# Gathering the last states of node groups by counts loaded into registers, in a seven-round graph network on one core

## The reference

```python
x = _layernorm(x + L0(x, edge_index))                        # normalised sum over the edges of a node
x = _layernorm(x + L1(x, edge_index, edge_attr_32, ...))     # two transformer convolutions, softmax per node
x = _layernorm(x + L2(x, weight, edge_weight1, src, dst, edge_type_16))   # relation matrices, weighted sum
x = _layernorm(x + L3(x, edge_index, W1, b1, W2, b2))        # three edge convolutions, maximum per node
```

## Time and profile before

| | us |
|---|---|
| median of 3 runs | 8052.2 (8051.64 to 8053.5) |
| the profiled execution | 8052.15 |
| its span, first to last instruction | 8050.2 |
| POOL busy | 5546.3 (69%) |
| PE busy (matmuls) | 4278.3 (53%) |
| DVE busy | 2503.7 (31%) |
| ACT busy | 2071.7 (26%) |

### The profile page before, as it was taken

One profiled execution on the slowest core, in us unless ns is written; L12 is line 12 of the kernel. 1 busy time (PEld: TensorE's weight loads), 2 busy tenths in 40 slices (PEclk: granted clock), 3 DMA queues, 4 the chain that ended last, 5 costly groups with the idle time before them and its releaser, 6 DMA issues.

```text
span 8050.2 us, 123362 instructions
## 1 busy us (share of the span) xinstructions
PE 4278.3 (53%) x24036; PEld 2775.3 (34%) x24036; DVE 2503.7 (31%) x4334; ACT 2071.7 (26%) x6406; POOL 5546.3 (69%) x5874
## 2 busy tenths in 40 slices
PE   3444435555555555566333326666646666466664
PEld 2333324444444444442222213333323333233332
DVE  5444435555535555531333331111111111111112
ACT  1111114444424444431111111111111111111111
POOL 6777757666637666633777757777767777577776
PEclk9999999999999999999999996565555656556565
DMA  5566647777736767622222224444444544344443
GB/s 144 150 150 150 150 102 151 150 151 151 152 87 151 152 152 151 149 61 93 60 59 59 59 60 109 111 112 112 101 96 112 112 111 111 86 112 111 111 111 87
DMA packets 2187581, 925.65 MB, mean 115 GB/s; under 512 B 1607262, under 2 KB 2070694, under 8 KB 2181094
## 3 DMA queue, kind: packets, MB, share of 16 engines
q1 hardware_dynamic: 1078982, 458.38, 23.1%
q10 hardware_dynamic: 921120, 272.38, 14.6%
q0 software_dynamic: 187392, 193.93, 13.3%
HBM read 657.22 MB, written 266.58 MB: 115 GB/s over the span
## 4 chain that ended last, share of the span: by engine, by line
PE 45%; issue 36%; POOL 9%; DVE 4%; DMA 4%; ACT 2%; ACTq 0%; DVEq 0%; POOLq 0%
POOL edges_a L906 8%; PE ps L1213 8%; PE ps L1205 7%; PE ps L1136 6%; PE ps L1132 6%; PE ps L1148 5%; PE ps L1197 4%; PE ps L1122 3%; DMA edges_a<-src_table,idx 3%; PE ps L584 2%; PE ps L1113 1%; PE ps L635 1%; PE ps L577 1%; POOL edges_a L913 1%; PE ps L1181 1%
## 5 line engine op out<-in xcount | busy, mean ns | idle before, releaser
L906 POOL DMA_INDIRECT edges_a<-src_table,idx x4040 | 3821.5, 946 | 1519.6 <-issue 1165.5
L913 POOL DMA_INDIRECT edges_a<-src_table,idx x1616 | 1524.6, 943 | 768.5 <-issue 448.8
L1341 DVE TENSOR_TENSOR_SCAN st<-pen,st,ps 128x512 f32<-128x512 f32 x300 | 383.9, 1280 | 2591.9 <-PE ps L1205 2591.7
L1132 PE MATMUL ps<-ident,edges_a 128*128 128x128 f32 x1212 | 563.5, 465 | 1173.1 <-issue 1024.6
L1213 PE MATMUL ps<-ident,st 64*128 64x64 f32 (+2 forms) x4444 | 926.2, 361 | 430.3 <-issue 395.1
L1122 PE MATMUL ps<-ident,edges_a 128*64 128x128 f32 x1616 | 419.1, 415 | 1255.1 <-DVE edges_a L1359 672.7
L1213 PEld LDWEIGHTS ps<-ident,st 64*128 64x128 f32 (+2 forms) x4444 | 704.9, 215 | 1043.9 <-issue 997.0
L1341 DVE TENSOR_TENSOR_SCAN st<-edges_a,st,ps 64x512 f32<-64x512 fp8e4 x402 | 511.2, 1272 | 874.9 <-issue 475.8
L1132 PEld LDWEIGHTS ps<-ident,edges_a 128*128 128x128 f32 x1212 | 219.3, 181 | 1428.8 <-issue 1266.4
L1040 ACT ACTIVATE edges_a<-ps,b 128x512 f32<-128x512 f32 x303 | 208.2, 687 | 1912.6 <-PE ps L1136 1912.6
L1122 PEld LDWEIGHTS ps<-ident,edges_a 128*64 128x64 f32 x1616 | 216.4, 158 | 1337.7 <-issue 1256.5
(11 more groups left out here) (189 smaller groups left out, 3531.6 us busy)
## 6 DMA issues: line engine op xcount, KB each, us to landing
states_sum<-hb ACTq DMA_DIRECT2D x1010, 128.0 KB
win_sb<-dst_table SPq DMA_DIRECT2D x1616, 72.8 KB
edges_a<-src_table,idx POOLq DMA_INDIRECT x5656
states_att<-hb ACTq DMA_DIRECT2D x404, 194.0 KB
win_sb<-dst_table ACTq DMA_DIRECT2D x1212, 48.0 KB
win_sb<-dst_table SPq DMA_DIRECT2D x1212, 48.0 KB
dst_b<-in_dst_row SPq DMA_DIRECT2D x50, 1024.0 KB, 5.7
sel<-onehots SPq DMA_DIRECT2D x303, 128.0 KB
```

What stands on the lines that cost most here:

```text
L906: pool.indirect_dma_start(rows[:, s, j * D:(j + 1) * D], None, srcs[q.r], bass.IndirectOffsetOnAxis(ap=idx[:, s, j:j + 1], axis=0))\
L913: pool.indirect_dma_start(xe_a[:, s, j * KA:j * KA + D], None, srcs[q.r], bass.IndirectOffsetOnAxis(ap=idx_a[:, s, j:j + 1], axis=0))\
L1132: nc.tensor.matmul(bank(TURNED, s)[:, at_j], rows[:, s, j * P:(j + 1) * P], ident[:, :], is_transpose=True, start=True, stop=False)
L1341: nc.vector.tensor_tensor_scan(st[0:w, s % V, :], d0, d1, init, op0, op1).then_inc(q.st_ready.sem, 1)
```

## The change

The change has three parts.

1. A table of counts. DVE makes `group_ends` with 17 small operations ahead of the masks: for each of the first six groups, how many rows of four chunks must be stored until the group's last edge is covered, times 16 (for MAX rounds times 32), once cut off at the larger and once at the smaller number of uses that a slot has in a round. For the halves of a MAX round a group of the first half needs its own rows, a group that reaches into the second half while it begins in the first needs all of them, and a group of the second half needs its rows there.
2. In rounds 2 to 6 POOL, in place of one wait ahead of the 25 gathers, loads two of these counts into registers ahead of each of the first six groups and waits for the four slots with them. Ahead of the last group it waits for all chunks, as before.
3. In rounds 0 and 1 POOL waits for all chunks ahead of group 0 as before (and again, in vain, ahead of group 6).

```diff
                 kw = KA if q.kind == ATT else D
-                for s in range(U):
-                    wait(pool, (q.st_stored[s], 16 * q.per_step * ((q.steps - s + U - 1) // U)))
+                each, most, least = 16 * q.per_step, -(-q.steps // U), q.steps // U
+                pool.wait_ge(ends_made, ENDS_MADE)
                 for g, (b0, nb) in enumerate(GROUPS):
+                    if g < G - 1 and q.r > 1:
+                        ends = [nc.values_load(group_ends[P - 1:P, int(q.kind == MAX), e:e + 1],
+                                               engines=[mybir.EngineType.Pool], min_val=each, max_val=each * m)
+                                for e, m in ((g, most), (G - 1 + g, least))]
+                        wait(pool, *[(q.st_stored[s], ends[0] if s < q.steps % U else ends[1]) for s in range(U)])
+                    elif g == G - 1 or not g:
+                        wait(pool, *[(q.st_stored[s], each * ((q.steps - s + U - 1) // U)) for s in range(U)])
                     for b in range(b0, b0 + nb):
...
+            half, full = float(CH * EC), float(-(-CH // U))
+            begins, finals = edges_le[:, 0:GB * (G - 1):GB], edges_le[:, GB:NB:GB]
...
+            for to, off in ((all_rows, 0.0), (second_rows, half)):
+                end_op(nc.vector.tensor_scalar(to, finals, -1.0 - off, 0.0, ALU.add, ALU.max))
+                end_op(nc.vector.tensor_scalar(to, to, 1.0 / (U * EC), 1.0, ALU.mult, ALU.add))
+                end_op(nc.vector.tensor_copy(up_to, to))
+                end_op(nc.vector.tensor_copy(to, up_to))
+            end_op(nc.vector.tensor_scalar(first_rows, finals, half, full, ALU.is_gt, ALU.mult))
+            end_op(nc.vector.tensor_tensor(first_rows, first_rows, all_rows, ALU.add))
+            end_op(nc.vector.tensor_scalar(split_rows, begins, half, full, ALU.is_le, ALU.mult))
+            end_op(nc.vector.tensor_tensor(second_rows, second_rows, split_rows, ALU.add))
+            end_op(nc.vector.tensor_tensor(second_rows, second_rows, first_rows, ALU.min))
+            for i, (of, steps, each) in enumerate(((all_rows, C, 16.0), (second_rows, CH, 32.0))):
+                for j, most in enumerate((-(-steps // U), steps // U)):
+                    end_op(nc.vector.tensor_scalar(group_ends[:, i, j * (G - 1):(j + 1) * (G - 1)], of, float(most), each,
+                                                   ALU.min, ALU.mult))
```

More of the change, by code:

```diff
@@ L133, in gnn_kernel @@
         dinv = sb("dinv", [P, NB])
+        group_rows = sb("group_rows", [P, 4, G - 1])
+        group_ends = sb("group_ends", [P, 2, 2 * (G - 1)], i32)
         xn = sb("xn", [P, NB, D])
@@ L231, in gnn_kernel @@
         agg_ready = [sem(f"agg_ready{g}") for g in range(G)]
+        ends_made = sem("ends_made")
         LN = ["sum", "mean", "centred", "square", "var", "rstd", "norm"]
@@ L427, in pre_tiles @@
             return 2 + sum(nb + 2 for _, nb in GROUPS[:g + 1]) + 3 * max(g - LATE + 1, 0)
+        ENDS_MADE = 17
         LATE = 3
@@ L1302, in _, with end_op @@
             assert made[0] == PRE_SCALED
+            done = [0]
+            def end_op(ins):
+                done[0] += 1
+                ins.then_inc(ends_made, 1)
+                dve.wait_ge(ends_made, done[0])
+            half, full = float(CH * EC), float(-(-CH // U))
+            begins, finals = edges_le[:, 0:GB * (G - 1):GB], edges_le[:, GB:NB:GB]
+            all_rows, first_rows, second_rows, split_rows = (group_rows[:, i, :] for i in range(4))
+            up_to = group_ends[:, 0, 0:G - 1]
+            for to, off in ((all_rows, 0.0), (second_rows, half)):
[12 more added lines that the diff above has]
+                                                   ALU.min, ALU.mult))
+            assert done[0] == ENDS_MADE
             nc.vector.tensor_copy(tile_last[:, 0:whole].unsqueeze(2), tile_dst[:, 0:whole, P - 1:P])
```

## The result

| | before | after |
|---|---|---|
| median of 5 runs, us | 8053.5 (8051.64 to 8054.84) | 8005.59 (8003.41 to 8006.57) |
| the profiled execution, us | 8052.15 | 8005.16 |
| its span, us | 8050.2 | 8003.2 |

The ratio is 0.9941, with an interval of 0.9926 to 0.9955: 48 us less, where 49.6 were forecast and the median of after lies 3 us above the forecast. None of them ran on the chip of the result, so what is said of that chip rests on the two traces, before and after.

A forecast was written before the change was run, and what follows sets the result against it. POOL's gathers of source rows pace the chunks; the change fills POOL's idle seams between rounds. Gains 12.5 + 9.2 + 9.5 + 9.5 + 8.9 = 49.6 us off 8052.2 gave 8002.6 us, range 7996.5 to 8015.

The forecast's parts named there:

- The forecast of 12.5 us: End of round 2: group 0 is gathered before the last scan ends, DVE's wait of 12.59 us goes, gain 12.5.
- I cost that at nothing: Round 2: gathers beside the last chunks' work take POOL and DMA engines that idled before, at cost nothing.
- The term of 0.84 us a pair: POOL, ahead of a group: two register loads at 0.42 us each, read from SP's gaps, add 0.84 us.
- The 8004: Skill's floor of about 600 ns a load: pair 1.2 us, sum below 1.5 us smaller, result about 8004.
- round 3's remaining wait: Seam of round 3: 0.77 of 10.36 us remain, plus 0.4 for a later landing; gain 9.2.
- round 6's late groups: Round 6: chain needs a group every 5.29 us, POOL gives one every 5.84; 0.6 of 9.5 lost, gain 8.9.
- Rounds 4 and 5: Seams of rounds 4 and 5: groups come early enough, all of the wait goes, gain 9.5 us each.
- The start: Start: 17 DVE operations take 3.4 us, but POOL's four chunks (20 us) of lead absorb it; 0, upper end 3.4.
- The loads don't pace POOL: Rival, chance 0.13: loads at 1.5 us each make a group 8 us on POOL; gain 38.4, time 8013.8.
- The last chunk doesn't land earlier: Rival, chance 0.12: each MAX round's last chunk lands up to 1.4 us earlier, 4.2 in all; time 7997.
- The start shows: Rival, chance 0.07: the table's 3.4 us at the start come on top; time 8006.
- The slower rival: Rival, chance 0.02: at 3 us a load POOL bounds the seams, 8074; gain and loss balance near 2.5 us.

The follow-up runs named there:

- constants: The change with this input's counts written as numbers in the waits, no register loads; 10391.79 us on chip 12, 1.0012 of the kernel before.
- table_only: The change without register loads, POOL waiting for all chunks ahead of group 0 as before; 10383.09 us on chip 12, 1.0005 of the kernel before.
- late_table: The change with its 17 DVE operations moved behind the rest of DVE's start; 10395.93 us on chip 12, 1.0012 of the kernel before.
- change_again: The change itself, unaltered, run on chip 8; 10444.56 us, 1.0007 of the kernel before.
- paced: The change with constant counts and four unneeded loads behind every early gather, rounds 2 to 6; 10254.74 us on chip 12, 1.0002 of the kernel before.

## Why the prediction was right, and what it left out

**What bounds the kernel, and round 2.** Right. The forecast of 12.5 us was 12.50 in the seam. The last scan starts 27.13 us behind the last gather of rows, against 26.87: "I cost that at nothing" for the gathers beside the last chunks' work was right on this chip. It is also the step that fails on the others: on chip 12 the same work took 58.9 us (constants) instead of 31.0 (table_only). The prediction never asked whether the other engines can issue while POOL gathers, and the trace of before had an answer for its own chip only: in that trace PE, DVE and ACT do run beside the late `agg` gathers. So the result holds for the chip of the result; the change gave 1.0007 on chip 8.

**The loads.** The term of 0.84 us a pair was too large; what shows is nothing, the lower bound that the prediction named and didn't take. The step that failed is the addition: a load's time was put on the chain of gathers, where it lies under them. The size of one load was about right: 0.47 us recorded, 0.57 from one to the next, against the 0.42 read from a gap on SP; what was wrong is where it was added. (The 8004 that the prediction gives by the price from the Trainium skill lies nearer to the measured 8005.6, but by luck, since that price too was added to the chain.) With the term went round 3's remaining wait (0.77, and 0.4 for landing) and round 6's late groups: 10.45 and 9.87 us instead of 9.2 and 8.9.

**Rounds 4 and 5.** 10.03 and 9.30 for 9.5 each.

**The start.** The term was 0 and its upper end 3.4; the last gather of rows of round 0 starts 3.1 us later. The 17 operations stand in the trace as costed (the first at 58.41, the last ending at 61.85), and the first one-hot starts 5.2 us later than before:

```profile
76.66 0.88 DVE L1387 TENSOR_SCALAR sel<-dst_b,nodes 128x128 fp8e4<-128x128 int32 x4 [6.29 <-DMA edges_a<-flags]
```

POOL's first gather of rows comes only 0.8 us later, and the rest appears within round 0, so the four chunks of lead seem not to have covered it. How much of the 3.1 us is the table's is not shown, since 2 us came and went within rounds 2 and 3 with no change there. Which of the delayed loads would hand it on is open too: table_only and late_table, made for this, ran on a chip where 3 us can't be told from no change.

**The rivals.** The loads don't pace POOL: no pitch of 8 us between groups. The last chunk doesn't land earlier: from the last gather of rows to the end of the last scan are 12.45, 13.10 and 12.27 us in rounds 4 to 6 against 12.24, 13.07 and 12.61, where 1.4 less each was claimed. "The start shows" is right in its size (3 of 3.4 us) but stood beside the full price of the loads. The two errors, loads too dear by 2 to 3 us and the start too cheap by 3, and 1.7 us more from there to the start of round 2 (0.9 of it in the seams of rounds 0 and 1), nearly cancel; the median came out 3 us above the forecast. That it is so near is luck in part: the seams gave 2.6 us more than forecast, and the rest of the span took 5.2. The slower rival asked for 2.5 us a load and more, over four times what a load takes.

## What to carry to other kernels

Work moved into an engine's idle time is free only if the others can still issue beside it; look in the trace for a stretch where both already run, and run the kernel on more than one chip before trusting a gain of half a per cent. Register loads between indirect gathers cost nothing here, as issuing them (0.5 to 0.6 us a load, by estimate 0.4 a gather) stayed below the gathers' own pitch. When a trace has no row for a price, ask also whether it lies on the chain at all. Where back-to-back gathers of POOL hold the rest back, a short pause between groups, here some 2 us for four gathers, was worth more than the time it took, and a pause behind every gather was too much.

## What was not expected of the hardware

**Chips differ by 27 to 30%.** The kernel before takes 8053 us on one chip and 10251 to 10466 on three others, with the same instructions and the same duration of a gather (0.94 us). The difference lies in what PE, DVE and ACT do while POOL gathers: on chip 12 no instruction in 10 us beside eight gathers. What it is in the chip that holds them back stays open; the rows above lead to PE first, which starts matmuls 1.5 to 2.1 us apart that wait for nothing, and whose signals come late. Where all stand still the DMA engines are busy for less than a quarter of the time. The Trainium skill (SBUF — State Buffer, section SBUF: two separate sides) knows an exclusive lock between DVE and GpSimd, by which either can block the other; among the examples is DVE keeping GpSimd from writing descriptors. PE and ACT never wait for it by that page, and PE stands still here too, so it doesn't explain these rows. The Trainium skill (Runtime: NRT & Kernel Launch, section Instruction fetch mechanics) says that the cost of fetching the next block of instructions is mostly hidden. The packets of these fetches are few and alike: the pages of after and of change_again both count 30 and 59 on the two queues that carry them, and one lies in the 30 us from 4814 to 4844 of constants. So nothing speaks for more fetching on these chips; whether an engine waits for instructions in another way no run tells.

One rival is untested. The traces of chips 8, 11 and 12 hold some 56800 to 58300 updates of semaphores, those of before and after 229400 to 229800, for nearly the same instructions. All times here are of recorded executions. Whether the recording differs between the chips, and itself holds the engines back on some, no run here shows; then the 27 to 30% would be no property of the kernel there.

**A clock row of 1.00 can be a missing row.** In the stretch from 3750 to 4700 us (round 3) the view of before has the upper level of TensorE's clock, 2.4 GHz, and that of after the lower, 1.2 GHz. Before, then after:

```profile
3750.00:4700.00 950.00, 313.56 (x1520) 196.64 (x1519) 322.17 (x379) 111.56 (x379) 718.66 (x760) 1.00 0.28 59
```
```profile
3750.00:4700.00 950.00, 314.48 (x1525) 197.26 (x1524) 322.51 (x381) 111.94 (x380) 718.33 (x761) 0.50 0.28 59
```

A matmul takes 313.56 / 1520 = 206 ns in the one and 314.48 / 1525 = 206 ns in the other, so it looks as if the clock had halved and nothing got longer. But where both levels are recorded within 25 us of one trace, they do make a difference. These are two matmuls of L1216 in change_again, first at the upper level, then at the lower (PE busy, weight loads, granted clock, DMA share, GB/s):

```profile
9307.00:9313.00 6.00, 1.12 (x2) 0.30 (x2) 1.00 0.40 93
9314.00:9330.00 16.00, 2.08 (x2) 0.50 (x2) 0.50 0.34 76
```

Equal matmuls in round 3 (the starts of those of L1122 before and L1133 after lie 213 ns apart in both traces, too) therefore say that PE ran at one level in both. The trace of before has no clock record at all ahead of 4843 us, and that of after none ahead of 2422 us, and such a stretch is shown as 1.00. Within after the matmuls of L1159 are 81 ns apart both in round 1 (shown as 1.00) and in round 2 (0.50). So the mean clocks of the two spans, 0.837 and 0.688, can't be compared, nor does the 1.00 in the windows of paced count, whose records begin at 6323 us. In rounds 4 to 6, where both traces have records, the clock is 0.59 in each. What the clock is worth to this kernel no run shows.
